# A fused language-model tower: side work of linear attention spread over its tiles, and another order of the matmuls in a tile

## The reference, cut to what matters

```python
h = log_softmax(causal_conv_tower(x))            # 6 layers of conv, gelu, pointwise
s = layernorm(h)
# linear attention, 8 heads
qs    = einsum('bti,hij->bhtj', s, Q)
Omega = einsum('bhtj,buj->bhtu', qs, s) * tril   # no softmax
es    = einsum('hij,buj->bhui', E, s)
h = h + einsum('bhtu,bhui->bti', Omega, es)
h = h + block(layernorm(h))   # rmsnorm, 4-head softmax attention, top-2 of 8 experts
```

## Time and profile before

| | |
|---|---|
| time, median of 3 runs | 254.31 us (253.91 to 254.62) |
| profiled execution, its own time | 255.38 us |
| its span, first to last instruction | 253.5 us |
| mean granted TensorE clock | 0.974 of full |
| instructions | 7312 |
| linear attention, tiles 0 to 15 | about 52 to 113 us of the span |

### The profile page before, as it was taken

The page is one execution under the profiler, slowest core; times in us unless marked ns, Lnnn a source line. Parts: engine busy times, 40 slices in busy tenths (PEclk is TensorE's granted clock), DMA queues, the critical chain, the costliest instruction groups (busy, mean ns, idle before and its releaser), DMA issues.

```text
span 253.5 us, 7312 instructions
## 1 busy us (share of the span) xinstructions
PE 211.7 (84%) x2828; PEld 137.2 (54%) x2836; DVE 173.6 (69%) x417; ACT 154.2 (61%) x277; POOL 145.0 (57%) x199
## 2 busy tenths in 40 slices
PE   8977889878788795896988898979799899889992
PEld 3644546355555454564666666754466466455661
DVE  4135656876484836749796687947977974999686
ACT  2478765567855574494555555568666578566670
POOL 6830000134565863377258887647789884876771
PEclk9999999999999999897699999999999999999997
DMA  2566200000000000000000000000000010000010
GB/s 44 122 153 172 71 3 3 3 0 3 4 3 0 3 3 0 3 5 0 3 0 3 0 3 0 4 3 1 3 3 1 0 23 4 0 20 3 3 23 21
DMA packets 8396, 4.51 MB, mean 18 GB/s; under 512 B 7556, under 2 KB 7852, under 8 KB 8364
## 3 DMA queue, kind: packets, MB, share of 16 engines
q1 hardware_dynamic: 8364, 4.06, 6.7%
HBM read 3.53 MB, written 0.52 MB: 16 GB/s over the span
## 4 chain that ended last, share of the span: by engine, by line
PE 35%; DVE 27%; issue 12%; ACT 10%; POOL 8%; SPq 6%; DMA 1%; DVEq 0%; POOLq 0%; ACTq 0%
PE bank L1367 33%; DVE shared L1328 2%; POOL stat L349 2%; DVE nmx L1118 2%; POOL oTx L486 1%; DMA w1s<-in_w1r_dram 1%; DVE L L1295 1%; POOL shared L419 1%; ACT early L665 1%; DVE oT L1148 1%; ACT qT L801 1%; ACT oT L650 1%; DVE nmr L1127 1%; DVE shared L958 1%; SPq L238 1%
## 5 line engine op out<-in xcount | busy, mean ns | idle before, releaser
L1367 PE MATMUL bank<-early 64*64 64x256 f32 (+5 forms) x556 | 58.2, 355 | 12.0 <-DVE early L848 3.0
L419 POOL TENSOR_TENSOR shared<-shared 128x512 f16<-128x512 f32 x44 | 51.3, 1165 | 17.2 <-ACT shared L786 14.5
L1367 PEld LDWEIGHTS bank<-early 64*64 64x64 f32 (+3 forms) x556 | 31.1, 127 | 30.4 <-ACT early L552 5.5
L1328 DVE SCALAR_TENSOR_TENSOR shared<-bank,qT 128x512 f32<-128x512 f32 x44 | 29.7, 688 | 12.4 <-ACT qT L801 11.8
L349 POOL TENSOR_TENSOR stat<-stat,neghalf 128x4 f32<-128x4 f32 x14 | 14.2, 1014 | 38.2 <-DVE stat L933 36.4
L786 ACT CAST shared<-shared 128x512 f16<-128x512 f32 x44 | 27.0, 614 | 12.1 <-DVE shared L1328 12.1
L801 ACT ACTIVATE qT<-bank 128x512 f32<-128x512 f32 x44 | 26.3, 597 | 10.5 <-PE bank L1367 10.3
L486 POOL TENSOR_TENSOR oTx<-oT,oTx 128x512 f16<-128x512 f32 x16 | 18.7, 1169 | 21.6 <-ACT oTx L656 21.5
L1367 PE MATMUL bank<-onehot,w3h 128*128 128x512 f16 x88 | 26.3, 380 | 3.6 <-DVE shared L1328 3.5
L1367 PE MATMUL bank<-qT,shared 64*64 64x128 f32 (+1 forms) x320 | 20.7, 337 | 9.1 <-DVE shared L958 5.7
L1367 PE MATMUL bank<-onehot,w1h 128*128 128x512 f16 x88 | 26.2, 380 | 0.3 <-ACT qT L801 0.3
(11 more groups left out here) (235 smaller groups left out, 452.4 us busy)
## 6 DMA issues: line engine op xcount, KB each, us to landing
early<-in_tcn_w_dram SPq DMA_DIRECT2D x2, 320.0 KB, 4.2
w1s<-in_w1m_dram SPq DMA_DIRECT2D x2, 256.0 KB, 3.6
qT<-in_w3m_dram SPq DMA_DIRECT2D x2, 256.0 KB, 3.5
out_dram<-L SPq DMA_DIRECT2D x8, 64.0 KB, 1.7
qw<-in_attn_q_dram SPq DMA_DIRECT2D x4, 64.0 KB, 2.5
hTs<-in_w2m_dram SPq DMA_DIRECT2D x1, 256.0 KB
cos<-in_cos_t_dram SPq DMA_DIRECT2D x2, 96.0 KB, 2.6
sin<-in_sin_t_dram SPq DMA_DIRECT2D x2, 96.0 KB, 2.1
```

Of the source, the lines that this page charges most:

```text
L419: nc.gpsimd.tensor_tensor(hhx[:, i, 1, :], hh[:, u % RING, :], hhx[:, i, 0, :], ALU.subtract).then_inc(S["lo_ready"], 1)
L1328: V_.scalar_tensor_tensor(hh[:, u % RING, :], bank[B_BANK[u % 2]][:, :], HH_SCALE / FFN_SCALE, sil[:, u % 2, :], ALU.mult, ALU.mult).then_ ...
L1367: return nc.tensor.matmul(out_, l_, r_, start=a, stop=z, skip_group_check=skip)
```

## The change

In a tile, TensorE's order becomes `omega(g + 1)`, `carried(g, 0)`, `project(g - 1)`, `carried(g, 1)`, `attend(g)`; before it was `carried(g, 0)`, `omega(g + 1)`, `carried(g, 1)`, `attend(g)`, `project(g - 1)`. The side work for a later pair is spread: for pairs 2 and 3 `prep` in the first tile of the pair before, two queries in the second and two in the third, the outer sums in the fourth (pair 1 keeps its queries in tile 2). ScalarE, VectorE and POOL follow the same places. `sTd`, `Ms` and the new `sd` (instead of `s2`) hold all four pairs. LN2 and the RMS scale of every pair are computed as before only for the last pair: two bases at once and one POOL power over both; the functions `last_centre`, `last_bases`, `last_rows` and `last_roots` become `second_centre`, `second_bases`, `second_rows` and `second_roots`, and `ln2_b`, `ln2_c`, `ln2_d` go. The diff, cut to its core:

```diff
-        s2 = sb("s2", [P, 2, 4, 2, V])
+        s2 = sb("s2", [P, 2, 4, V])
         shared = sb("shared", [P, 12288])
-        sTd = shared[:, 0:1024].rearrange("p (x t) -> p x t", x=2)
-        Ms = shared[:, 1024:1792].rearrange("p (x b k u) -> p x b k u", x=2, k=3, u=C)
+        sTd = shared[:, 0:2048].rearrange("p (x t) -> p x t", x=PAIRS)
+        Ms = shared[:, 2048:3584].rearrange("p (x b k u) -> p x b k u", x=PAIRS, k=3, u=C)
+        sd = shared[:, 3584:5632].rearrange("p (x a d v) -> p x a d v", x=PAIRS, a=4, d=2)
...
-        QUERY_BANK = ((2, 3, 2, 3), (3, 0, 3, 0), (3, 0, 3, 0), (0, 0, 0, 1))
+        QUERY_BANK = ((2, 3, 2, 3), (3, 0, 3, 0), (3, 0, 3, 0), (0, 1, 0, 1))
...
-                inverse_root(12, 11, p, "var2_ready", "rstd2_ready")
-            def last_roots():
-                g4 = slice(TILES - 4, TILES)
-                pool.wait_ge(S["var2_ready"], PAIRS)
+            def second_roots(p):
+                g4 = slice(4 * p, 4 * p + 4)
+                pool.wait_ge(S["var2_ready"], p + 1)
                 nc.gpsimd.tensor_tensor(stat[:, 13:15, g4], stat[:, 11:13, g4],
                                         neghalf[:, 0:4].unsqueeze(1).to_broadcast([P, 2, 4]), ALU.pow) \
                     .then_inc(S["rstd2_ready"], 1)
...
-                    first_split(p + 1)
-                if s == 0 and p >= 2:
-                    second_split(p - 2)
+                if g == 0:
+                    first_split(1)
+                if g == 2:
+                    variance_root(2)
+                if g == 3:
+                    first_split(2)
                 if g == 4:
                     first_h(0)
-                if s == 1 and p:
-                    first_h(p)
-                if s == 2 and p:
-                    variance2_root(p - 1)
-                if s == 3:
-                    if p:
-                        square2_root(p - 1)
-                    if p + 2 < PAIRS:
-                        variance_root(p + 2)
+                    variance_root(3)
+                if g == 5:
+                    first_h(1)
+                if g == 6:
+                    first_split(3)
+                if g == 7:
+                    second_roots(0)
+                if g == 8:
+                    second_split(0)
+                if g == 9:
+                    first_h(2)
+                if g == 11:
+                    second_roots(1)
+                    first_h(3)
+                if g == 12:
+                    second_split(1)
+                if g == 14:
+                    second_roots(2)
+            low_rows(TILES - 1)
             second_split(2)
-            low_rows(TILES - 1)
             pair_parts(1)
-            last_roots()
+            second_roots(3)
...
                 p, s = g // 4, g % 4
-                if s == 2 and p + 1 < PAIRS:
+                if g == 2:
+                    q_out(1, 0)
+                o_out(g)
+                if g in (1, 4, 8):
+                    sixteen_turned(g // 4 + 1)
+                    turned_rows(g // 4 + 1)
+                if g == 1:
+                    exponentials(2)
+                    exponentials(3)
+                if g == 2:
+                    q_out(1, 1)
+                    q_out(1, 2)
+                    q_out(1, 3)
+                if g in (9, 13):
+                    h_rows(p - 2)
+                if g in (5, 9):
                     q_out(p + 1, 0)
-                o_out(g)
-                if s == 1 and p + 1 < PAIRS:
-                    sixteen_turned(p + 1)
-                    turned_rows(p + 1)
-                if s == 1 and p >= 2:
-                    h_rows(p - 2)
+                    q_out(p + 1, 1)
+                if g in (6, 10):
+                    q_out(p + 1, 2)
+                    q_out(p + 1, 3)
+                if g in (3, 7, 11):
+                    outer_out(p + 1)
                 if g == 13:
                     first_copies()
-                if s == 2 and p + 1 < PAIRS:
-                    q_out(p + 1, 1)
-                    outer_out(p + 1)
-                    q_out(p + 1, 2)
-                    q_out(p + 1, 3)
-                if g == 2:
-                    exponentials(2)
-                    exponentials(3)
                 if g == 3:
                     act.wait_ge(S["lsum_ready"], PAIRS)
                     nc.scalar.activation(stat[:, 1, :], stat[:, 0, :], ACT.Ln).then_inc(S["ln_ready"], 1)
                 if g >= TILES - 2:
                     stacked(2 * (g - TILES + 2))
                     stacked(2 * (g - TILES + 2) + 1)
-                if g == 11:
+                if g == 12:
                     nc.scalar.activation(warm[:, :], vcol[:, :], ACT.Exp)
...
             def ln0_c(p):
                 g4 = slice(4 * p, 4 * p + 4)
                 dve.wait_ge(S["rstd_ready"], p + 1)
-                if p >= 2:
-                    dve.wait_ge(S["shl_ready"], max(p - 2, 1))
-                    dve.wait_ge(S["o_ps"], 4 * (p - 1))
-                V_.tensor_tensor(s2[:, p % 2, :, :, :], cen[:, p % 2, :, :].unsqueeze(2).to_broadcast([P, 4, 2, V]),
+                V_.tensor_tensor(sd[:, p, :, :, :], cen[:, p % 2, :, :].unsqueeze(2).to_broadcast([P, 4, 2, V]),
...
-            def ln2_b(p):
+            def second_centre(p):
+                g4 = slice(4 * p, 4 * p + 4)
+                h_ = h[:, g4, :]
                 if p:
                     dve.wait_ge(S["hr_ready"], p)
-                centre(p, h[:, 4 * p:4 * p + 4, :], cenB[:, :, :], sqrB[:, :, :], 11, "var2_ready")
-            def last_centre():
-                g4 = slice(TILES - 4, TILES)
-                h_ = h[:, g4, :]
-                dve.wait_ge(S["hr_ready"], 3)
                 link(V_.tensor_reduce(stat[:, 2, g4], h_, AX, ALU.add))
                 V_.scalar_tensor_tensor(cenB[:, :, :], bc4(stat[:, 2, g4]), -1.0 / V, h_, ALU.mult, ALU.add) \
-                    .then_inc(S["cen3_ready"], 1)
-            def last_bases():
-                g4 = slice(TILES - 4, TILES)
-                dve.wait_ge(S["cen3_ready"], 1)
+                    .then_inc(S["cen2_ready"], 1)
+            def second_bases(p):
+                g4 = slice(4 * p, 4 * p + 4)
+                dve.wait_ge(S["cen2_ready"], p + 1)
                 link(V_.tensor_tensor(sqrB[:, :, :], cenB[:, :, :], cenB[:, :, :], ALU.mult))
                 link(V_.tensor_reduce(stat[:, 9, g4], sqrB[:, :, :], AX, ALU.add))
                 link(V_.tensor_scalar(stat[:, 11, g4], stat[:, 9, g4], 1.0 / V, 1e-5, ALU.mult, ALU.add))
...
-            def last_rows():
-                g4 = slice(TILES - 4, TILES)
-                dve.wait_ge(S["rstd2_ready"], PAIRS)
-                link(V_.tensor_tensor(xf[:, g4, :], cenB[:, :, :], bc4(stat[:, 13, g4]), ALU.mult))
-                dve.wait_ge(S["hsplit_ready"], PAIRS - 1)
-                V_.tensor_tensor(hrB[:, :, :], xf[:, g4, :], bc4(stat[:, 14, g4]), ALU.mult) \
-                    .then_inc(S["hr_ready"], 1)
-            def ln2_c(p):
+            def second_rows(p):
                 g4 = slice(4 * p, 4 * p + 4)
                 dve.wait_ge(S["rstd2_ready"], p + 1)
-                link(V_.tensor_tensor(xf[:, g4, :], cenB[:, :, :], bc4(stat[:, 12, g4]), ALU.mult))
-                link(V_.tensor_tensor(stat[:, 10, g4], stat[:, 12, g4], stat[:, 12, g4], ALU.mult))
-                link(V_.tensor_tensor(stat[:, 10, g4], stat[:, 10, g4], stat[:, 9, g4], ALU.mult))
-                V_.tensor_scalar(stat[:, 5, g4], stat[:, 10, g4], 1.0 / V, 1e-6, ALU.mult, ALU.add) \
-                    .then_inc(S["q1_ready"], 1)
-            def ln2_d(p):
-                g4 = slice(4 * p, 4 * p + 4)
-                dve.wait_ge(S["rinv_ready"], p + 1)
+                link(V_.tensor_tensor(xf[:, g4, :], cenB[:, :, :], bc4(stat[:, 13, g4]), ALU.mult))
                 if p:
                     dve.wait_ge(S["hsplit_ready"], p)
-                V_.tensor_tensor(hrB[:, :, :], xf[:, g4, :], bc4(stat[:, 6, g4]), ALU.mult) \
+                V_.tensor_tensor(hrB[:, :, :], xf[:, g4, :], bc4(stat[:, 14, g4]), ALU.mult) \
                     .then_inc(S["hr_ready"], 1)
             def rotary(p):
...
                 V_.tensor_copy(d_[:, :, 4:6, 1, :], t6[:, :, 4:6, :]).then_inc(S["parts0_ready"], 1)
+            def exact_parts_end():
+                t6 = rot[:, :, :].rearrange("p a (n e) -> p a n e", e=HD)
+                d_ = qst[:, 0, :, :, :, :]
                 dve.wait_ge(S["parts0_ready"], 3)
                 V_.tensor_tensor(d_[:, :, 0:4, 5, :], t6[:, :, 0:4, :], d_[:, :, 0:4, 3, :], ALU.subtract) \
                     .then_inc(S["split_ready"], 1)
...
                 mask_omega(g)
+                if g == 0:
+                    ln0_c(1)
                 if g == 1:
                     ln0_a(2)
                     exp_sum(0)
+                    ln0_a(3)
                     exp_sum(1)
-                    ln0_a(3)
                 if g == 2:
                     ln0_b(2)
                 if g == 3:
```

(83 more changed lines are left out.)

35 lines of the change are left out of this document (15 added, 20 removed).

## The result

The changed kernel took 259.24 us (median of 4 runs, 258.43 to 260.17); the kernel before took 254.34 us beside it (4 runs, 253.91 to 254.62). The ratio is 1.0195 with a 95% interval of 1.0158 to 1.0233, so it is slower, by 4.9 us against a forecast of 2.2. An execution more than 1.5% above the fastest of its kernel is left out of medians and intervals; that happened once (254.41 us, Omega first). The profiled execution took 258.43 us with a span of 256.5 (before: 255.38 and 253.5).

The account below looks back on a forecast made before the run. The prediction took linear attention's tiles with side work to bind the old kernel. Its terms, +3.8 (stage), +0.4 (contention) and -2.0 (seam), gave +2.2 us: 256.5 us on the median's scale, range 252 to 260.

Parts of the forecast that it names:

- the loop: In linear attention, o_out copy through ScalarE and POOL's low part to projection and the next copy: 3.9 us a tile.
- the likeliest case: The loop as worked out binds in linear attention: 255 to 258.5 us, chance 0.50.
- Contention: In linear attention VectorE's LN2 work, sharing SBUF interfaces, stretches POOL's low part L486: +0.4 us, ends 0 and 2.9.
- Side work under the wait: Between an o_out copy and the projection at 2.55 us, side work fitting in about 1.7 us costs nothing.
- The excesses: Delays beyond the wait: tile 2 +0.35 us, tile 3 +1.5, tiles 7 and 11 +0.6 each, tile 0 +0.25.
- The seam and the clock: Between linear and softmax attention, less idle time and a higher granted clock take off 2.0 us, ends 0 and 2.6.
- the gap: TensorE's 1.85 us wait for rotary(1) before softmax attention goes; maxima split ends 5.4 us after the last L650, gaining 1.2.
- so 257.6 on that run's scale and 256.5 on the median's: The whole sum, +2.2 us on the profiled run, carried to the median, which lay 1.07 us below that run.
- The +3.8: Last o_out copy of linear attention 3.8 us later, at 116.0 where it was 112.20; bounds +0.8 and +6.8.
- A: In linear attention the wait for the low part never ends last: faster, named 251 us, chance 0.23.
- B: A draw: the loop near its short end, +0.8 to +2, the seam 1.2 to 1.6: 253.5 to 255 us, chance 0.14.
- C: The loop binds and idle TensorE in tiles without side work loses granted clock: +3 to +4 us, 260, chance 0.13.

Follow-up runs that it names:

- Omega first: The spread alone with carried(g, 0) moved behind Omega and nothing else; 251.95 us, ratio 0.9896.
- the spread alone: The changed kernel with the old order in a tile; side work spread, LN2 and buffers as changed; 246.16 us, ratio 0.9688.
- before filled: The kernel before with dummy bf16 matmuls in TensorE's two long waits (40 in tile 12, 30 before the second scores for the maxima); 253.50 us, ratio 0.9957.

## Why the prediction was half right

The direction and the mechanism of the loop came true. The size did not: 259.24 us lies inside the stated 252 to 260, but above the 255 to 258.5 of the likeliest case, and the loss is 4.9 us, not 2.2.

Put on a grid, the four medians are:

| | old order | new order | order costs |
|---|---|---|---|
| old placement | 254.3 | 269.6 | +15.3 |
| new placement | 246.2 | 259.2 | +13.1 |
| placement gives | -8.1 | -10.4 | |

With the second measurement of the change (261.2) the last column reads +15.0 and the last row -8.4; the signs and the order of size stay.

**The loop: right.** Every point named was found. L481 releases TensorE before the projection, the plain tile takes 3.91 to 3.94 us (3.9), tiles 7 and 11 4.49 (4.5), tile 3 5.38 (5.4), tile 2 4.49 (4.25; its query waits 1.05 us for the copy of sTs). The fifteen distances make 62.41 us against 61.6. The last copy starts 4.78 us later than before; the terms for the stage were 3.8 and 0.4. Halving the low part showed the cause: 0.46 us a tile, 5.4 over the distances and 6.1 in all. The loop is most of the +13.1, not all that the order does: Omega first without the projection between the halves costs 3.7 to 5.8 us against the spread alone, for other reasons (the mask and TensorE's own semaphore), which do not simply add to the loop's.

**Contention: right in size.** L481 takes 1.155 us in the median and 1.388 at its longest; two instances lie above, 1.28 in tile 0 and 1.39 in tile 12, 0.36 us together against the 0.4 taken; the distances to tiles 1 and 13 are 4.06 and 4.17 where the other plain tiles have 3.91 to 3.97. The group's rows:

```profile
L481 POOL TENSOR_TENSOR oTx<-oT,oTx x16: 1152/1155/1388, 55.9 to 118.4; 128x512 f16<-128x512 f32 x16
...
  PE bank L1369: 11.1, 12
```

**Side work under the wait: right, but only half of the question.** The excesses that were named came out within 0.25 us. What the sum never asked is what the spread would give without the new order. It put the old waits for the mask, 5.7 us, at nothing because the loop had replaced them. It also read their cause from the list of waits as LN2's second power; with that power gone the wait stayed at 6.7 us. The grid says that the placement is worth 8 us in the old order.

**The seam and the clock: the step that failed.** The sum took -2.0 us, of which 1.2 for the gap and 0.8 for the clock. On the profiled pair this looks right: the span grew by 3.0 us where the last copy moved by 4.8, so 1.8 came back behind it. But filling the waits of the kernel before gives 1.4 of these 1.8 without the change (141.3 to 139.9 us from last copy to end), and only 0.4 are left for it (139.5). Of the gap's 1.2 us, 1.0 is there: the split of the maxima begins 4.23 us behind the last copy, 5.24 in before filled, 5.36 before. Then 0.6 are lost again, because its subtraction L1129 now runs beside POOL (0.78 us, 0.17 in before filled). So the split ends 5.71 us behind the copy against 6.07 filled and 6.66 before: at a full clock the seam is worth 0.4 us, where I had taken 1.2 for the gap alone.

What failed is the step "so 257.6 on that run's scale and 256.5 on the median's". It took the profiled run's 1.07 us off both kernels alike, after the sum had won the clock's part back once. The profiled execution of before (mean granted clock 0.974) lay 1.0 us above its median, that of after (0.995) 0.8 below its own; the pair differs by 3.05, the medians by 4.9. At the median the two kernels have the same clock: 0.985 in the last group's runs of before, 0.987 in the eight runs of after. So the medians show no clock won. Between executions at a full clock the change costs 5.1 us: the copies take 62.41 us against 56.76, less 0.4 behind them and 0.2 ahead of the first, which is the difference of the spans, 256.5 and 251.4. The runs agree: 258.43 us at 0.995 against 253.06 to 253.50 for before filled. The +3.8, too, was measured from a profiled stage of before that held 1.3 us of idle time and low clock which filling removes. Where the changed kernel loses clock in its own typical run was seen once, at 128 to 136; the rest stays open.

**Rivals.** A, that side work covers the wait, is out: the loop shows in eleven of the fifteen distances, and the other four wait for the copies of sTs or q. But its condition, the gain of the spread, is real once the order is undone. B, a draw, is out by the interval. C put the clock's fall in the stage; two profiles (0.995 and 0.993) show 1.00 from 52 to 118, behind pauses of up to 1.58 us. In the two experiments with Omega first and no projection between the halves the granted clock fell right behind a wait of 1.97 us. The executions of the change at 0.979 to 0.987 were not profiled, so C is out for the two that were seen and not for these.

## What to carry to other kernels

Before moving a consumer ahead of other work on an in-order engine, walk the dependency from that engine's result, through the other engines, back to the moved instruction. If the work behind it feeds the next round of the same walk, the walk's length becomes the round's length, and no filling helps: only a shorter walk or the old order does. Judge the two halves of such a change apart, since a loss of 13 us can hide a gain of 8. And before a sum from one profiled execution is set against the medians, find out what its own clock and waits cost: here filling two waits took 2.1 us off the span of the profiled execution and 1.0 off the median.
